# A node loop's edge products two trips behind, with the split in two buffers and the sum in mid-trip

## The chip, the core and the metric

One NeuronCore of a Trainium2 chip runs the whole kernel. The metric is the time of one execution on the device, in microseconds (us). Engines: PE is TensorE (PEld its weight loads), DVE is VectorE, ACT is ScalarE, POOL is GpSimd, SP is SyncE, which here only issues transfers (SPq). L1472 is line 1472 of the kernel's file.

## The reference

Two layers of a graph network on 100,000 nodes of 64 features and 50,000 edges, fp32. Cut to what matters:

```python
h = relu(layernorm(x))
agg = segment_sum(h[src] * edge_weight[:, None], dst)
x = x + agg @ W_neigh + b_neigh + h @ W_self.T
seg_sum, seg_max, cnt = ...        # of edge_attr (32 wide), over src
seg_mean = seg_sum / max(cnt, 1);  seg_max = where(cnt > 0, seg_max, 0)
h = relu(concat([seg_sum, seg_max, seg_mean, u]) @ W1 + b1)   # hidden width 128
out = x + h @ W2 + b2
```

(The layer norm of the second layer enters nothing: that layer's result depends on the edges' attributes alone.)

## The kernel before, in words

The first three fifths of the program rank the edges, sort them by their source into windows of 128 nodes, gather the source nodes and make the messages; the change does not touch them. They leave in DRAM, for each window of 128 nodes, up to 96 slots of edge attributes sorted by source, per-slot flags, the messages sorted by destination (as three bf16 parts of each fp32 number, whose sum is the number), and x plus its own part.

The node loop (L1389 to L1646) then makes the output. It has WG = 98 trips; a trip g handles GT = 8 windows, 1024 nodes. Each engine runs its own program, and semaphores (`w[...]`) order them. Loads go through rings of four buffers (RING = 4), most other buffers exist once or twice. In trip g:

- SP (L1392 to L1403) loads x of the windows (L1399, one transfer) and eight chunks of messages (L1403, eight transfers), as soon as the buffers of trip g-4 are free: for x that is the semaphore "y" (the sum of g-4 made), for the chunks "picked" (their products made).
- POOL (L1408 to L1422) loads attributes, slots and flags.
- DVE: `permute(g+1)` (L1432, a one-hot of the slots), `value_left(g-1)` (L1478), `picks(g)` (L1460, L1462, the one-hot that adds messages into nodes), `value_low(g-1)` (L1484), `select(g)` (L1450, the one-hot that takes each node's last slot), `scans(g+1)` (L1441, L1442, L1444: running sum, running maximum and mean), `finish(g-1)` (L1472: y = x + PSUM).
- PE: `hidden(g)` (L1554, 24 fp32 products with W1), `permute(g+1)` (L1543), `edges(g-1)` (L1589), `outer(g)` (L1565 and L1568, the products with W2, called output or outer products here), `neighbours(g)` (L1579, the messages).
- ACT: `value_mid(g-1)` (L1633), `relu(g)` (L1622), `store(g-2)` (L1616, issues the store of y), `value_high(g)` (L1629).

The outer products leave an fp32 value in PSUM for each slot. It is split in three bf16 parts, high by ACT, what is left by DVE (`v_left`), mid by ACT, low by DVE, into one buffer `v_part`; then `edges` adds the parts, by 24 selecting products with the one-hot `sel`, to the same PSUM bank (two of them, by g % 2) in which `neighbours(g)` has already put the messages. `finish` reads that bank. So one window's value runs L1568, L1629, L1478, L1633, L1484, L1589, L1472 over two trips, and PE's queue has `edges(g-1)` ahead of `outer(g)`.

The order of the work is written out by hand: the order of calls in each engine's loop. The lines that wait, as they stand:

```python
def neighbours(g):                       # PE
    pe.wait_ge(w["pick"], g + 1)
    if g >= 2:
        pe.wait_ge(w["y"], g - 1)        # the bank's last sum
def select(g):                           # DVE
    if g >= 2:
        dve.wait_ge(w["o_ps"], g - 1)    # sel[g % 2] is read by edges(g-2)
```

Of the kernel before, what the change touches and what calls it, by code (L numbers as in the profile page):

```python
# [17 lines left out]
GT = 8  # L18
# [50 lines left out]
def graph_layers(nc, x, src, dst, attr, weight, w_neigh, b_neigh, w_self, u, w1, b1, w2, b2, out):  # L69
    N, D = x.shape  # L70
# [31 lines left out]
    with ctx:  # L102
# [518 lines left out]
        def parts_of(row):  # L621
            return row.bitcast(BF16).rearrange("p k (s c) -> p k s c", s=PARTS)
# [62 lines left out]
        def self_of(g):  # L685
            return s0_d[g * (GT * P):(g + 1) * (GT * P), :].rearrange("(p k) c -> p k c", p=P)
# [671 lines left out]
        sums, tops, means = (part_of(arena, P, 2 * SL) for _ in range(3))  # L1358
        hid = part_of(arena, P, GT * SL)
        v_left = part_of(arena, SL, GT, D)  # L1360
        v_part = parts_of(part_of(arena, SL, GT, KEY))
        one_hot = [part_of(arena, P, GT, P).rearrange("p k c -> p (k c)").bitcast(BF16)
                   .rearrange("p (n k c) -> p n k c", n=2, c=P) for _ in range(2)]
        sel = [one_hot[b][0:SL, 0, :, :] for b in range(2)]
# [24 lines left out]
        with nc.Block() as block:  # L1389
            @block.sync  # L1390
            def _(sp):

                at = [sp.alloc_register(f"at{k}") for k in range(GT)]
                for g in range(WG):
                    b = g % RING
                    sp.reg_load(at, starts[0:1, 0, g * GT:g * GT + GT])
                    if g >= RING:
                        sp.wait_ge(w["y"], g - RING + 1)
                    sp.dma_start(x_in[b][:, :, :], self_of(g)).then_inc(x_loaded[b], 16)  # L1399
                    if g >= RING:  # L1400
                        sp.wait_ge(w["picked"], g - RING + 1)
                    for k in range(GT):
                        sp.dma_start(chunk[b][0:CH, k, :], message[bass.ds(sp.snap(at[k]), CH), :]).then_inc(ch_loaded[b], 16)  # L1403

            @block.gpsimd
            def _(pool):
# [18 lines left out]
            def _(dve):  # L1425
# [49 lines left out]

                def value_left(g):
                    dve.wait_ge(w["high"], g + 1)
                    nc.vector.tensor_tensor(v_left[:, :, :], ps[v_bank][0:SL, :].rearrange("p (k c) -> p k c", c=D),  # L1478
                                            v_part[:, :, 0, :],
                                            ALU.subtract).then_inc(w["left"], 1)  # L1480

                def value_low(g):
                    dve.wait_ge(w["mid"], g + 1)
                    nc.vector.tensor_tensor(v_part[:, :, 2, :], v_left[:, :, :], v_part[:, :, 1, :],  # L1484
                                            ALU.subtract).then_inc(w["v"], 1)

                def c0_rows():
# [27 lines left out]
                for g in range(WG):  # L1515
                    if g + 1 < WG:
                        permute(g + 1)
                    if g >= 1:
                        value_left(g - 1)
                    picks(g)  # L1520
                    if g >= 1:
                        value_low(g - 1)
                    select(g)
                    if g + 1 < WG:
                        scans(g + 1)
                    if g >= 1:
                        finish(g - 1)
                value_left(WG - 1)
                value_low(WG - 1)
                finish(WG - 1)  # L1530

            @block.tensor
            def _(pe):
# [49 lines left out]
                def edges(g):  # L1583
                    c = g % 2
                    pe.wait_ge(w["sel"], g + 1)
                    pe.wait_ge(w["v"], g + 1)
                    for k in range(GT):
                        for n in range(PARTS):
                            last = nc.tensor.matmul(ps[o_bank[c]][:, D * k:D * k + D], sel[c][:, k, :], v_part[:, k, n, :],  # L1589
                                                    start=False, stop=(k == GT - 1 and n == PARTS - 1))  # L1590
                    last.then_inc(w["o_ps"], 1)

# [2 lines left out]
                for g in range(WG):  # L1595
                    hidden(g)
                    if g + 1 < WG:
                        permute(g + 1)
                    if g >= 1:
                        edges(g - 1)  # L1600
                    outer(g)
                    neighbours(g)
                edges(WG - 1)

            @block.scalar
            def _(act):
# [17 lines left out]

                def value_high(g):
                    act.wait_ge(w["v_ps"], g + 1)
                    if g >= 1:
                        act.wait_ge(w["o_ps"], g)
                    nc.scalar.activation(v_part[:, :, 0, :], ps[v_bank][0:SL, :].rearrange("p (k c) -> p k c", c=D), ACT.Copy).then_inc(w["high"], 1)  # L1629

                def value_mid(g):
                    act.wait_ge(w["left"], g + 1)
                    nc.scalar.activation(v_part[:, :, 1, :], v_left[:, :, :], ACT.Copy).then_inc(w["mid"], 1)  # L1633

                for g in range(WG):
                    if g >= 1:
                        value_mid(g - 1)
                    relu(g)
                    if g >= 2:
                        store(g - 2)  # L1640
                    value_high(g)
                value_mid(WG - 1)
                store(WG - 2)
                store(WG - 1)
                for b in range(RING):
# [241 lines left out]
```

## Time and profile before

| | us |
|---|---|
| median of 3 runs | 1773.02 (1772.13 to 1776.54) |
| the profiled execution | 1769.93 |
| its span in the trace | 1768.0 |
| first to last relu of the node loop (L1622, 98 of them) | 1086.9 to 1746.5 |
| PE busy over the whole span | 1081.4 (61%) |
| DVE busy over the whole span | 1390.8 (79%) |

The trace is of one execution; its busy times are of instructions, and an instruction's time on PE and DVE can overlap the start of the next by some hundredths of a microsecond, so that from start to start is shorter than the duration. The granted clock (PEclk) is 1.00 at TensorE's level of 2.4 GHz and 0.50 at 1.2 GHz. The first 1060 us belong to the parts that are not touched.

### The profile page before, as it was taken

The page shows a single profiled execution, that of the slowest core. Times are in us where ns is not written, and L with a number is a line of the kernel's source. Part 1 is how long each engine was busy: PE and PEld are TensorE (multiplying, and loading weights), DVE is VectorE, ACT ScalarE, POOL GpSimd, SP SyncE. Part 2 cuts the span into 40 slices and gives each one's busy share as a digit, 9 for nine tenths or more (in the row PEclk, how much of TensorE's full clock was granted, in tenths as well). Part 3 has the DMA queues.
Part 4 walks back from the last instruction along what each step waited for, and adds up shares of the span by engine and source line. Part 5 has one row for each costly group of instructions (what it writes and reads, how often), then busy time and mean ns, then how long its engine had stood idle before and what let it go on. Part 6 is the DMA issues. An engine that isn't in the chain of part 4 may idle for free. (4 is left out here: it accounts for less than half of the span.)

```text
span 1768.0 us, 39354 instructions
## 1 busy us (share of the span) xinstructions
PE 1081.4 (61%) x13658; PEld 933.2 (53%) x13659; DVE 1390.8 (79%) x3220; ACT 679.9 (38%) x1766; POOL 1104.8 (62%) x1407
## 2 busy tenths in 40 slices
PE   3266666666651023333333344898989998999996
PEld 2155555555551023332233333777877777777775
DVE  6599999999981056766667666888888988888886
ACT  2278888888840012222222221333333333333332
POOL 7777777777777777777777755444444444444440
PEclk9777788888865555555555556888788888878787
DMA  9944545454531053344432226878887878787882
GB/s 289 169 115 116 128 113 128 115 129 114 130 101 42 15 128 96 104 111 106 108 103 71 85 84 166 211 203 206 198 211 194 211 195 206 206 201 201 203 204 61
DMA packets 433690, 255.33 MB, mean 144 GB/s; under 512 B 373693, under 2 KB 381117, under 8 KB 432813
## 3 DMA queue, kind: packets, MB, share of 16 engines
q1 hardware_dynamic: 283198, 144.42, 33.7%
q0 software_dynamic: 46976, 72.79, 15.8%
q10 hardware_dynamic: 103312, 35.54, 8.0%
q8 instruction: 112, 1.84, 0.4%
q14 instruction: 92, 0.75, 0.1%
HBM read 164.15 MB, written 88.42 MB: 143 GB/s over the span
## 5 line engine op out<-in xcount | busy, mean ns | idle before, releaser
L850 POOL DMA_INDIRECT xg_all<-in_x_dram,idx_src x391 | 397.9, 1018 | 120.1 <-issue 118.9
L856 POOL DMA_INDIRECT by_win<-rows,idx_win x391 | 388.1, 993 | 128.1 <-issue 127.2
L1185 PE MATMUL ps<-ident,h 128*128 128x128 f32 x588 | 139.9, 384 | 279.0 <-DVE h L999 204.9
L1413 POOL DMA_DIRECT2D rows<-by_win x98 | 67.7, 691 | 353.9 <-DVE arena L1444 333.2
L1271 ACT ACTIVATE sq<-xc 128x512 f32<-128x512 f32 x147 | 92.6, 630 | 472.5 <-DVE xc L962 472.4
L1185 PEld LDWEIGHTS ps<-ident,h 128*128 128x128 f32 x588 | 94.7, 198 | 298.9 <-DVE h L999 218.2
L951 DVE TENSOR_REDUCE stat<-xg_all 128x8 f32<-128x512 f32 x49 | 33.4, 682 | 230.4 <-DMA xg_all<-in_x_dram,idx_src 230.3
L1418 POOL DMA_DIRECT2D rows<-flag_d x392 | 193.6, 501 | 12.2 <-issue 12.2
L1289 ACT ACTIVATE h<-xc,stat 128x64 f32<-128x64 f32 x784 | 196.3, 332 | 0.0
L1629 ACT ACTIVATE arena<-ps 96x512 bf16<-96x512 f32 x98 | 58.0, 592 | 332.9 <-PE ps L1568 238.1
L1568 PE MATMUL ps<-w_sb,arena 128*96 128x64 f32 x1568 | 184.1, 281 | 0.0
L1568 PEld LDWEIGHTS ps<-w_sb,arena 128*96 128x96 f32 x1568 | 168.9, 192 | 22.5 <-issue 22.5
L1554 PE MATMUL ps<-arena,w1r 32*128 32x192 f32 x2352 | 159.5, 413 | 9.2 <-DVE arena L1444 9.2
L1198 PE MATMUL ps<-wsT,hT 128*128 128x128 f32 x784 | 148.8, 353 | 1.3 <-DVE zeros L1012 0.8
L1198 PEld LDWEIGHTS ps<-wsT,hT 128*128 128x128 f32 x784 | 139.6, 266 | 2.5 <-issue 2.1
L1589 PE MATMUL ps<-arena 96*128 96x64 bf16 x2352 | 94.7, 201 | 66.9 <-DVE arena L1484 66.9
L1554 PEld LDWEIGHTS ps<-arena,w1r 32*128 32x128 f32 x2352 | 123.4, 234 | 16.0 <-issue 9.6
L1589 PEld LDWEIGHTS ps<-arena 96*128 96x128 bf16 x2352 | 84.7, 104 | 88.1 <-issue 87.9
L1478 DVE TENSOR_TENSOR arena<-ps,arena 96x512 f32<-96x512 f32 x98 | 67.3, 687 | 75.6 <-ACT arena L1629 73.0
L445 PE MATMUL ps<-ones_b,same 128*128 128x1 bf16 x392 | 17.0, 164 | 176.9 <-DVE pos_f L350 176.6
L1462 DVE TENSOR_TENSOR arena<-iota_n,arena 96x1024 bf16<-96x1024 f32 x98 | 119.6, 1221 | 3.4
L1622 ACT ACTIVATE arena<-ps,hbias 128x768 f32<-128x768 f32 x98 | 88.2, 900 | 85.0 <-PE ps L1554 85.0
(209 smaller groups left out, 2580.4 us busy)
## 6 DMA issues: line engine op xcount, KB each, us to landing
rows<-message SPq DMA_DIRECT2D x784, 36.4 KB, 3.3
rows<-flag_d POOLq DMA_DIRECT2D x392, 72.0 KB, 3.6
rows<-s_d SPq DMA_DIRECT2D x98, 256.0 KB, 2.9
out_dram<-rows ACTq DMA_DIRECT2D x97, 256.0 KB
message<-m_row SPq DMA_DIRECT2D x48, 388.0 KB, 2.4
arena<-in_x_dram SPq DMA_DIRECT2D x70, 256.0 KB, 3.4
s_d<-arena SPq DMA_DIRECT2D x70, 256.0 KB, 2.2
zeros<-slot_d POOLq DMA_DIRECT2D x98, 144.0 KB, 3.3
```

The lines of the kernel that those rows point to most:

```text
L850: nc.gpsimd.indirect_dma_start(out=xg[g % RX][:, t % GT, :], out_offset=None, in_=x, in_offset=bass.IndirectOffsetOnAxis(ap=idx_src[:, t:t ...
L856: nc.gpsimd.indirect_dma_start(out=by_win, out_offset=bass.IndirectOffsetOnAxis(ap=idx_win[0:parts, t:t + 1], axis=0), in_=rows[0:parts, t ...
L1185: last = nc.tensor.transpose(hT_of[n % 2][:, P * k:P * k + P], h[n % 2][:, 2 * k:2 * k + 2, :].rearrange("p a c -> p (a c)"), ident[:, :])
L1198: last = nc.tensor.matmul(bank[:, P * k:P * k + P], hT[n % 2][:, k, :], weights[:, :], start=True, stop=True)
L1271: nc.scalar.activation(sq[:, :, :], xc[n % 2][:, :, :], ACT.Square).then_inc(ln["squared"], 1)
L1289: last = nc.scalar.activation(h[b][:, k, :], xc[b][:, k, :], ACT.Relu, scale=stat[b][:, 2, k:k + 1])
L1418: pool.dma_start(f_in[b][DE * q:DE * q + DE, :, :].rearrange("p f s -> p (f s)"), two.unsqueeze(0).to_broadcast([DE, 3 * 2 * SL])).then_in ...
L1462: nc.vector.tensor_tensor(pick[c][0:CH, :, :], iota_n[0:CH, :].unsqueeze(1).to_broadcast([CH, GT, P]), near[c][:, :].unsqueeze(2).to_broad ...
L1554: last = nc.tensor.matmul(ps[z_bank[q]][:, 0:2 * SL], w1r[DE * q:DE * q + DE, j, :], part[DE * q:DE * q + DE, :], start=(j == 0), stop=(j ...
L1568: last = nc.tensor.matmul(ps[v_bank][0:SL, D * k:D * k + D], hid[:, SL * k:SL * k + SL], w2_sb[:, :], start=False, stop=(k == GT - 1))
L1589: last = nc.tensor.matmul(ps[o_bank[c]][:, D * k:D * k + D], sel[c][:, k, :], v_part[:, k, n, :], start=False, stop=(k == GT - 1 and n == ...
L1622: nc.scalar.activation(hid[:, :].rearrange("p (q c) -> p q c", q=4), z_ps, ACT.Relu, bias=hbias[:, :]).then_inc(w["hid"], 1)
```

## The change

`edges` runs two trips behind instead of one: in trip g PE makes the selecting products of g-2, at the same place in its order. `v_part` becomes two buffers, by g % 2, so ACT's value_high(g) waits for the products of g-2 rather than g-1, and DVE's value_left(g) also waits for "v" of g-1, since `v_left` is still one buffer. DVE's `finish` runs for g-2, and stands after value_low and before select instead of at the end of the trip. ACT stores g-3 rather than g-2. SP issues the chunks ahead of x. After the loop stand edges(WG-2), finish(WG-2) and store(WG-3) in addition.

```diff
--- before.py
+++ after.py
@@ -1358,7 +1358,7 @@
         sums, tops, means = (part_of(arena, P, 2 * SL) for _ in range(3))
         hid = part_of(arena, P, GT * SL)
         v_left = part_of(arena, SL, GT, D)
-        v_part = parts_of(part_of(arena, SL, GT, KEY))
+        v_part = [parts_of(part_of(arena, SL, GT, KEY)) for _ in range(2)]
         one_hot = [part_of(arena, P, GT, P).rearrange("p k c -> p (k c)").bitcast(BF16)
                    .rearrange("p (n k c) -> p n k c", n=2, c=P) for _ in range(2)]
         sel = [one_hot[b][0:SL, 0, :, :] for b in range(2)]
@@ -1395,12 +1395,12 @@
                     b = g % RING
                     sp.reg_load(at, starts[0:1, 0, g * GT:g * GT + GT])
                     if g >= RING:
-                        sp.wait_ge(w["y"], g - RING + 1)
-                    sp.dma_start(x_in[b][:, :, :], self_of(g)).then_inc(x_loaded[b], 16)
-                    if g >= RING:
                         sp.wait_ge(w["picked"], g - RING + 1)
                     for k in range(GT):
                         sp.dma_start(chunk[b][0:CH, k, :], message[bass.ds(sp.snap(at[k]), CH), :]).then_inc(ch_loaded[b], 16)
+                    if g >= RING:
+                        sp.wait_ge(w["y"], g - RING + 1)
+                    sp.dma_start(x_in[b][:, :, :], self_of(g)).then_inc(x_loaded[b], 16)
 
             @block.gpsimd
             def _(pool):
@@ -1475,13 +1475,15 @@
 
                 def value_left(g):
                     dve.wait_ge(w["high"], g + 1)
+                    if g >= 1:
+                        dve.wait_ge(w["v"], g)
                     nc.vector.tensor_tensor(v_left[:, :, :], ps[v_bank][0:SL, :].rearrange("p (k c) -> p k c", c=D),
-                                            v_part[:, :, 0, :],
+                                            v_part[g % 2][:, :, 0, :],
                                             ALU.subtract).then_inc(w["left"], 1)
 
                 def value_low(g):
                     dve.wait_ge(w["mid"], g + 1)
-                    nc.vector.tensor_tensor(v_part[:, :, 2, :], v_left[:, :, :], v_part[:, :, 1, :],
+                    nc.vector.tensor_tensor(v_part[g % 2][:, :, 2, :], v_left[:, :, :], v_part[g % 2][:, :, 1, :],
                                             ALU.subtract).then_inc(w["v"], 1)
 
                 def c0_rows():
@@ -1520,13 +1522,14 @@
                     picks(g)
                     if g >= 1:
                         value_low(g - 1)
+                    if g >= 2:
+                        finish(g - 2)
                     select(g)
                     if g + 1 < WG:
                         scans(g + 1)
-                    if g >= 1:
-                        finish(g - 1)
                 value_left(WG - 1)
                 value_low(WG - 1)
+                finish(WG - 2)
                 finish(WG - 1)
 
             @block.tensor
@@ -1586,7 +1589,7 @@
                     pe.wait_ge(w["v"], g + 1)
                     for k in range(GT):
                         for n in range(PARTS):
-                            last = nc.tensor.matmul(ps[o_bank[c]][:, D * k:D * k + D], sel[c][:, k, :], v_part[:, k, n, :],
+                            last = nc.tensor.matmul(ps[o_bank[c]][:, D * k:D * k + D], sel[c][:, k, :], v_part[c][:, k, n, :],
                                                     start=False, stop=(k == GT - 1 and n == PARTS - 1))
                     last.then_inc(w["o_ps"], 1)
 
@@ -1596,10 +1599,11 @@
                     hidden(g)
                     if g + 1 < WG:
                         permute(g + 1)
-                    if g >= 1:
-                        edges(g - 1)
+                    if g >= 2:
+                        edges(g - 2)
                     outer(g)
                     neighbours(g)
+                edges(WG - 2)
                 edges(WG - 1)
 
             @block.scalar
@@ -1624,22 +1628,23 @@
 
                 def value_high(g):
                     act.wait_ge(w["v_ps"], g + 1)
-                    if g >= 1:
-                        act.wait_ge(w["o_ps"], g)
-                    nc.scalar.activation(v_part[:, :, 0, :], ps[v_bank][0:SL, :].rearrange("p (k c) -> p k c", c=D), ACT.Copy).then_inc(w["high"], 1)
+                    if g >= 2:
+                        act.wait_ge(w["o_ps"], g - 1)
+                    nc.scalar.activation(v_part[g % 2][:, :, 0, :], ps[v_bank][0:SL, :].rearrange("p (k c) -> p k c", c=D), ACT.Copy).then_inc(w["high"], 1)
 
                 def value_mid(g):
                     act.wait_ge(w["left"], g + 1)
-                    nc.scalar.activation(v_part[:, :, 1, :], v_left[:, :, :], ACT.Copy).then_inc(w["mid"], 1)
+                    nc.scalar.activation(v_part[g % 2][:, :, 1, :], v_left[:, :, :], ACT.Copy).then_inc(w["mid"], 1)
 
                 for g in range(WG):
                     if g >= 1:
                         value_mid(g - 1)
                     relu(g)
-                    if g >= 2:
-                        store(g - 2)
+                    if g >= 3:
+                        store(g - 3)
                     value_high(g)
                 value_mid(WG - 1)
+                store(WG - 3)
                 store(WG - 2)
                 store(WG - 1)
                 for b in range(RING):
```

## Rows read from the trace of the kernel before

**Rows 1.** One stretch of the loop, PE: us, busy (x instructions), PEclk, DMA share, GB/s

```profile
1100.00:1750.00 650.00, 584.83 (x9991) 0.83 0.79 199
```

**Rows 2.** Waits in 1100 to 1750 us: total us, times, longest

```profile
PE ps L1589 <- DVE arena L1484: 65.3, 63, 1.5
```

**Rows 3.** Timeline, DVE, one trip: start us, us, engine, line

```profile
1423.77 0.69 DVE L1478 TENSOR_TENSOR arena<-ps,arena 96x512 f32<-96x512 f32 x1
...
1425.70 0.68 DVE L1484 TENSOR_TENSOR arena<-arena 96x512 bf16<-96x512 f32 x1
1426.31 1.21 DVE L1450 TENSOR_TENSOR arena<-iota_n,end_n 96x1024 bf16<-96x1024 f32 x1
...
1428.60 0.68 DVE L1472 TENSOR_TENSOR rows<-rows,ps 128x512 f32<-128x512 f32 x1
1429.20 0.62 DVE L1432 TENSOR_SCALAR arena<-zeros,row_n 96x768 f32<-96x768 bf16 x1
```

**Rows 4.** Timeline, DVE, before the loop

```profile
1073.74 0.62 DVE L1432 TENSOR_SCALAR arena<-zeros,row_n 96x768 f32<-96x768 bf16 x1 [12.26 <-DMA rows<-flag_d]
1074.28 0.18 DVE L1488 CAST arena<-c0b 128x64 bf16<-128x64 f32 x1
```

**Rows 5.** Timeline, PE, a trip at the full level and the start of the next

```profile
1421.54 1.57 PE L1568 MATMUL ps<-w_sb,arena 128*96 128x64 f32 x16
...
1423.78 1.26 PE L1554 MATMUL ps<-arena,w1r 32*128 32x192 f32 x24
1424.97 0.54 PE L1543 MATMUL ps<-arena,rows 96*32 96x96 f32 x16
1426.53 0.86 PE L1589 MATMUL ps<-arena 96*128 96x64 bf16 x24 [1.03 <-DVE arena L1484]
...
1427.66 2.21 PE L1568 MATMUL ps<-w_sb,arena 128*96 128x64 f32 x16
```

**Rows 6.** Timeline, ACT, the same trip

```profile
1423.14 0.59 ACT L1629 ACTIVATE arena<-ps 96x512 bf16<-96x512 f32 x1 [3.27 <-DVE rows L1472]
...
1425.11 0.90 ACT L1622 ACTIVATE arena<-ps,hbias 128x768 f32<-128x768 f32 x1
```

**Rows 7.** Stretches of one clock level, PE, columns as in rows 1

```profile
1414.74:1421.56 6.82, 5.79 (x119) 1.00 0.76 200
1421.56:1428.39 6.83, 5.80 (x114) 1.00 0.76 185
1428.39:1435.22 6.83, 6.83 (x95) 0.50 0.80 218
```

**Rows 8.** Timeline, PE, at the low level

```profile
1431.08 2.30 PE L1554 MATMUL ps<-arena,w1r 32*128 32x192 f32 x24
1433.32 0.87 PE L1543 MATMUL ps<-arena,rows 96*32 96x96 f32 x16
...
1749.08 2.70 PE L1568 MATMUL ps<-w_sb,arena 128*96 128x64 f32 x16
1751.58 1.49 PE L1579 MATMUL ps<-rows,arena 97*128 97x64 bf16 x24
1754.67 1.44 PE L1589 MATMUL ps<-arena 96*128 96x64 bf16 x24 [1.60 <-DVE arena L1484]
```

**Rows 9.** Timeline, DVE: the sum L1472 of single trips

```profile
1163.17 0.68 DVE L1472 TENSOR_TENSOR rows<-rows,ps 128x512 f32<-128x512 f32 x1
...
1435.57 0.69 DVE L1472 TENSOR_TENSOR rows<-rows,ps 128x512 f32<-128x512 f32 x1
...
1442.81 0.68 DVE L1472 TENSOR_TENSOR rows<-rows,ps 128x512 f32<-128x512 f32 x1
...
1709.33 0.67 DVE L1472 TENSOR_TENSOR rows<-rows,ps 128x512 f32<-128x512 f32 x1
```

**Rows 10.** SP: the chunks of one trip (timeline), and their landing (page)

```profile
1423.72 4.05 SPq L1403 DMA_DIRECT2D rows<-message  x8
...
rows<-message SPq DMA_DIRECT2D x784, 36.4 KB, 3.3
```

## The prediction

> **What bounds the kernel now.** I read the page first, for where the loop stands: it is the last two fifths of its slices, where DVE and PE are both nearly full and the clock's digits swing. Then the busy time over 650 us of the loop: PE works 585 us of them, nine tenths, at a mean granted clock of 0.83 [rows 1]. No engine is full, so I asked who waits for whom: the selecting products (L1589) wait 63 times, about 1.03 us each, for DVE's last part of the split, L1484 [rows 2].
>
> The timeline of one trip at the full level shows both loops that could set 6.13 us (from one DVE sum, L1472, to the next). One is DVE's own work: from L1478 to the next L1432 it is 5.43 us with no gap [rows 3]; L1432 itself, seen where nothing holds its successor, is 0.54 us from start to start [rows 4]. That makes 5.97. The other is the chain of one window's value: L1484 to L1589 0.83 us, L1589 to L1568 1.13, L1568 to ACT's L1629 1.60, on to L1478 0.63, and over the picks to L1484 1.93 [rows 3, 5, 6]. That makes 6.12. So the chain binds, and DVE stands still some 0.16 us in a trip. PE has 5.11 us of work in it (6.13 less the idle 1.02 between L1543's end and L1589).
>
> Then the clock. It moves between its two levels, 1.2 and 2.4 GHz, in stretches; a low one of 6.83 us lies between high ones, mostly of twice that length. In a high stretch PE is busy 5.8 of 6.83 us, in a low one all of it [rows 7]. At the low level hidden (L1554) takes 2.24 us from start to start for 1.19, the outer products 2.70 us in duration for 1.57, and the whole of PE's trip, by the durations of the low rows, 8.9 us (1.49 + 2.24 + 0.87 + 1.44 + 0.35 for L1565 + 2.50 for L1568) [rows 5, 8]. One low stretch costs two trips 14.21 us for 12.26: 1.95 us [rows 9]. A mean clock of 0.83 says that 34% of the loop is low, so 650 us hold 32 such stretches, about 63 us; 6.13 us a trip plus that gives 6.80, and the trips have it. The loop is thus 0.16 us a trip of chain and about 0.67 of clock above DVE's own 5.97.
>
> One number more decides the forecast. Eighty trips from 1163.17 to 1709.33 take 546.16 us [rows 9]: 6.827 each, equal to the length of the clock's shortest stretch to a part in a thousand. A mean over trips of 6.13, 6.97 and 7.24 has no reason to hit that number unless the trips are held in step with the clock's changes: they run ahead at 6.13, come to stand so that the clock falls, lose 2 us and stand right again.
>
> **The change, part by part.** The selecting products of window g-2 in trip g: their split was finished a trip before, so the 1.02 us of waiting goes, and the chain of the value is cut. What is late next at the full level is DVE: 5.97. The gain there is 0.16 x 97 trips = 15.5 us. The bounds: nothing, if the permutation's 0.54 can't be had here; a few us more, if the waits behind finish cost less.
>
> The sum (L1472) moves to mid-trip and now waits for products of the same trip. Count from L1432's start: left at 0.54, low at 2.47, finish at 3.08, select 3.68, end 5.97, the scans' result at 6.05 [rows 3, 4]. PE starts hidden 0.15 later as it does after L1484 now, at 0.23 of the next trip, then permute at 1.42, the selecting products 1.96 to 2.82: the sum finds them 0.2 us early. Queued behind it are select and the scans, and PE's next hidden waits for those. If the low level falls on that piece: 0.23 + 2.24 + 0.80 + 1.44 = 4.71 [rows 5, 8], the sum is 1.68 us late, with all behind it; working through the next trip gives some 0.2 more. So a low stretch costs about 1.9 us in the new order too, against 1.95 now: the cost changes its place (the chain's wait at L1478 before, the sum after), not its size.
>
> The outer products need hidden's relu: hidden ends 1.42, ACT's mid part ends at about 1.9, relu 0.90 [rows 6] to 2.8, where PE is ready at the same time, so 0 to 0.15 us in PE's slack. neighbours(g) now waits for the sum of the same trip, done at 3.76; PE gets there at 4.5. The second buffer of the split: value_high waits for the products of g-2, which stand ahead of its own input; value_left's wait is for DVE's own earlier work: each nothing, at most 0.05 us of issue, 5 us in all if it were exposed. Covers: PE's place in its queue, and DVE's own order.
>
> SP: the eight transfers of the chunks go ahead of the one of x, and the wait for y behind them. SP's chunks need 4.05 us of a 6 us trip [rows 10]. After the change the sum it waits for (g-4) stands in the middle of trip g-2, so the chunks of g+1 go out from 4.3 of trip g-2 to 2.5 of trip g-1, land 3.3 later [rows 10], and are read at 1.15 of g+1: over a trip spare. x is read a trip later than now. The store (g-3 for g-2) finds its sum done; the old image of y is wanted two and a half trips after. Price: nothing, with a trip of cover on each. POOL's loads hang on permute and scans, which keep their places. At the end one more group of products and one more sum stand behind the last trip, in a PE gap of 1.60 us against their 1.44 [rows 8]: 0 to +0.7 us.
>
> **The sum.** By the trips alone: -15.5 (chain) - 1 (low stretches) + 0.5 (end) = -16. By the trips in step with the clock: a fast trip of 5.97 runs ahead sooner, the clock falls sooner, and it pays until the mean is 6.83 again. That takes 97 x (6.80 - 5.97) / 1.9 = 42 low stretches in the place of 33; nothing is left but where the steps begin and end: -1.5, between -7 and +4. I take this one, since [rows 9] show the step held over 80 trips with an accuracy that a cost per trip would not give. The profiled execution was 1769.93 us with a span of 1768.0; the median of the runs is 1773.02, 3.1 above, and I put the difference on that: 1771.5.
>
> On the clock a page has a say. The rows: in high stretches PE is idle for one gap of about 1.02 us a trip, and the clock falls all the same [rows 5, 7]. The Trainium skill, TensorE: Matmul & The Clock Gate, in its section on the HAM oscillation that comes from cycling through PSUM, says that short idles between groups of products are enough to make the clock swing, and that throughput goes in the swings; these rows agree. Taken further, that rule speaks for the change (fewer idles, fewer falls) and gives the last rival below.
>
> **The rivals.**
> In step (0.52): 1771.5. For it: 6.827. Against: a step that held with 6.13 need not hold with 5.97.
> DVE has no 0.16 to give (0.05): L1432 costs 0.70 in every trip, the fast trip stays 6.13: 1773. Against: [rows 4].
> The clock falls as often as now (0.23): about 33 low stretches, each at 1.9, and fast trips of 5.97: 1757, 1753 to 1760. For it: mean busy shares of PE hardly change. Against: [rows 9].
> The clock is low half the time (0.14): as after some high stretches now, every single high stretch of 6.83 us is followed by a low one, and the sum in mid-trip takes the full loss each time. In 13.65 us then stand (13.65 - 1.95) / 5.97 = 1.96 trips, 6.96 us a trip: 0.14 to 0.16 more than now, 97 times, 1787. It decides from two things together: a mean clock of 0.75 and over 1.75 us lost in a low stretch; at 1.7 it is 6.83 and no change. PE's place is L1589, behind hidden and permute at the low level; DVE's is the wait of L1472, with select and scans queued behind it. A half-paid form is 1778.
> The clock falls less (0.06): idle drops from 1.02 to 0.86 us (5.97 - 5.11) in two pieces. With 22 low stretches: -15.5 - 11 x 1.95 = -37: 1736. The section named above would point here; the chance is small since the idle is hardly less.
>
> **How the numbers follow.** About 0.3%, 5.3 us, is what can be told from no change. In step: 0.42 same, 0.08 faster, 0.02 slower; no 0.16: 0.05 same; falls as now and falls less: 0.29 faster; half low: 0.14 slower. Faster 0.37, same 0.47, slower 0.16. The range takes in the in-step case, the case of unchanged falls and the lighter half of the low-half case: 1755 to 1780; in-step alone would be 1766 to 1777.
>
> **What would show it.** Right: fast trips between two L1472 of 5.97 to 6.0; no wait of L1589 for L1484; new waits of L1472 for L1589; a mean trip of 6.83; mean clock in the loop down from 0.83 to about 0.78. Wrong: mean clock 0.83 with 6.65 us a trip (falls as now), fast trips of 6.13, a trip above 6.9 with the clock at 0.75, or SP's chunks on DVE's list of waits.

## The result, and the profile after

The changed kernel takes 1692.29 us (median of 4, 1687.28 to 1702.37), against 1772.58 of the kernel before: a ratio of 0.955, interval 0.950 to 0.960. That is 80 us less, where the forecast was 1771.5 with a range of 1755 to 1780, in which the change would be paid back by TensorE's clock.

The windows view of the loop, PE alone (us, busy with instructions, granted clock, DMA share, GB/s), answers to [rows 1]:

```profile
1100.00:1680.00 580.00, 500.73 (x10080) 0.99 0.89 222
```

The granted clock is 0.99 where it was 0.83. The clock's line of the page shows it over the whole program: the last two fifths are the loop.

```profile
PEclk9678787787777555555555556599999999999998
```

The timeline of PE in one trip answers to [rows 5]:

```profile
1395.04 1.26 PE L1557 MATMUL ps<-arena,w1r 32*128 32x192 f32 x24 [0.72 <-DVE arena L1444]
1396.23 0.54 PE L1546 MATMUL ps<-arena,rows 96*32 96x96 f32 x16
1396.70 0.87 PE L1592 MATMUL ps<-arena 96*128 96x64 bf16 x24
1397.62 0.41 PE L1568 MATMUL ps<-arena 3*96 3x512 bf16 x1
1397.96 1.57 PE L1571 MATMUL ps<-w_sb,arena 128*96 128x64 f32 x16
1399.37 0.90 PE L1582 MATMUL ps<-rows,arena 97*128 97x64 bf16 x24
1400.99 1.26 PE L1557 MATMUL ps<-arena,w1r 32*128 32x192 f32 x24 [0.72 <-DVE arena L1444]
```

(Lines have moved: hidden is L1557, permute L1546, the selecting products L1592, the outer products L1568 and L1571, neighbours L1582.) The wait ahead of the selecting products is gone. PE's idle now stands in front of hidden, 0.72 us, where it waits for DVE's scans; the trip is 5.95 us, as both L1557 rows show. DVE's sum over the whole loop, the lines view of L1472, answers to [rows 9]:

```profile
L1472 DVE TENSOR_TENSOR rows<-rows,ps x98: 674/676/689, 1101.8 to 1681.7; 128x512 f32<-128x512 f32 x98
```

579.9 us for 97 trips, 5.98 each, against 659.4 before (1096.7 to 1756.1). The whole gain is in the loop. POOL's wait in the rows below stood there before. New are PE's wait for the scans and 13 waits of DVE's picks for a load of messages (late loads, from here on); what the forecast had as the likely new wait, the sum for its products, stays small:

```profile
POOL rows L1413 <- DVE arena L1444: 268.3, 88, 4.2
...
PE ps L1557 <- DVE arena L1444: 72.3, 94, 1.3
...
DVE arena L1460 <- DMA rows<-message: 5.8, 13, 1.3
DVE rows L1472 <- PE ps L1592: 1.9, 2, 1.0
```

Some runs below came to chips on which the parts ahead of the loop take 300 us longer, for every kernel; there the ratios are diluted, and the loop alone (first to last sum) is compared.

### The profile page after: what moved, and what is told of

Its sections match the earlier page's. It is cut to its first block and busy times, and to the rows that moved or that the text cites. A ratio compares the mean times of both kernels' runs of the same rounds, so it can differ in the third digit from the quotient of the medians.

```text
span 1693.7 us, 39358 instructions
## 1 busy us (share of the span) xinstructions
PE 988.4 (58%) x13658; PEld 841.2 (50%) x13659; DVE 1381.0 (82%) x3220; ACT 670.9 (40%) x1766; POOL 1090.5 (64%) x1407
## 5 line engine op out<-in xcount | busy, mean ns | idle before, releaser
L1413 POOL DMA_DIRECT2D rows<-by_win x98 | 51.2, 522 | 300.7 <-DVE arena L1444 279.6
L1557 PE MATMUL ps<-arena,w1r 32*128 32x192 f32 x2352 | 127.2, 347 | 82.3 <-DVE arena L1444 82.3
L1571 PE MATMUL ps<-w_sb,arena 128*96 128x64 f32 x1568 | 155.2, 252 | 0.0
L1571 PEld LDWEIGHTS ps<-w_sb,arena 128*96 128x96 f32 x1568 | 141.7, 166 | 22.5 <-issue 22.5
L1557 PEld LDWEIGHTS ps<-arena,w1r 32*128 32x128 f32 x2352 | 97.6, 190 | 94.5 <-DVE arena L1444 84.8
L1637 ACT ACTIVATE arena<-arena 96x512 bf16<-96x512 f32 x98 | 61.8, 631 | 192.2 <-DVE arena L1480 192.2
L1450 DVE TENSOR_TENSOR arena<-iota_n,end_n 96x1024 bf16<-96x1024 f32 x98 | 118.9, 1213 | 0.0
L445 PEld LDWEIGHTS ps<-ones_b,same 128*128 128x128 bf16 x392 | 14.2, 101 | 182.9 <-issue 182.4
L969 DVE TENSOR_REDUCE stat<-sq 128x8 f32<-128x512 f32 x147 | 99.5, 677 | 2.1 <-ACT sq L1271 2.1
```

What stands on the lines that cost most here:

```text
L969: nc.vector.tensor_reduce(stat[n % 2][:, 3, :], sq[:, :, :], AX, ALU.add).then_inc(ln["summed"], 1)
L1450: nc.vector.tensor_tensor(sel[g % 2][:, :, :], iota_n[0:SL, :].unsqueeze(1).to_broadcast([SL, GT, P]), end_n[:, g * GT:g * GT + GT].unsque ...
L1557: last = nc.tensor.matmul(ps[z_bank[q]][:, 0:2 * SL], w1r[DE * q:DE * q + DE, j, :], part[DE * q:DE * q + DE, :], start=(j == 0), stop=(j ...
L1571: last = nc.tensor.matmul(ps[v_bank][0:SL, D * k:D * k + D], hid[:, SL * k:SL * k + SL], w2_sb[:, :], start=False, stop=(k == GT - 1))
```

## Experiments

### Is the clock the gain? Products that do nothing, in the gap of the kernel before

```diff
                 def edges(g):
                     c = g % 2
+                    if g >= 1:
+                        pe.wait_ge(w["y"], g)
+                    for _ in range(24):        # b_fill24; 8 in b_fill8
+                        nc.tensor.matmul(ps[o_bank[1 - c]][:, 0:D], identb[:, :], identb[:, 0:D], start=True, stop=True)
```

> The kernel before with 24 more bf16 products in PE's gap ahead of the selecting products (results thrown away; they fill about 0.8 of the 1.03 us). Theory G (what changed is PE's idle gap, and with it the granted clock): PE's idle per trip falls under that of the changed kernel, the clock stays high, the chain still gives 6.13 us a trip: mean clock in the loop over 0.97, about 1708 us. Rival S (the order of the queues itself brought the gain: DVE no longer waits on the value): more work on PE brings nothing or costs at the low level: 1773 or up to 1800 us, mean clock 0.83 or less.

> The same with 8 products (0.27 us of the gap filled, 0.75 left, about the changed kernel's 0.72 of one gap). Theory G: if it is the length of the gap or the idle share (12% of a trip) that decides, the clock stays high mostly: 1710 to 1730 us. Rival: 1773 and a mean clock of 0.83.

Measured: 1708.59 us (0.965, 0.963 to 0.966) with 24 and 1705.81 (0.962, 0.961 to 0.964) with 8. With more work on PE the kernel before is 63 and 66 us faster. The windows rows of the loop, with 24 and with 8 products:

```profile
1100.00:1680.00 580.00, 558.32 (x12193) 1.00 0.87 222
```

```profile
1100.00:1680.00 580.00, 514.66 (x10697) 1.00 0.88 223
```

The clock is 1.00, and the fast trip stays at the chain's 6.13 us. With 8 products 0.69 us of idle is left in the old place:

```profile
1408.96 0.86 PE L1593 MATMUL ps<-arena 96*128 96x64 bf16 x24 [0.69 <-DVE arena L1484]
```

So of the 80 us, 66 are the clock and the 13.5 that are left between 1705.8 and 1692.3 are the chain.

### Idle given back to the changed kernel

A fill is a write that nobody reads, on DVE.

```diff
                     if g + 1 < WG:
                         scans(g + 1)
+                    nc.vector.memset(prod[:, 0:4, :], 0.0)      # a_hold_s; 0:8 in a_hold_l
```

> The changed kernel with a DVE fill of 128 elements behind the scans in each trip (0.1 to 0.2 us, which lengthens PE's gap by as much: 0.85 to 0.9 us, a trip of about 6.1). By its own time it costs 10 to 18 us: 1702 to 1710. Theory G: near the edge of the kernel before (1.03 us of gap, 6.13 us trip), clock falls may come back: anything up to 1760. Rival S: 1702 to 1710, clock as in the changed kernel.

> The same with 256 elements (0.25 to 0.3 us a trip; PE's gap 1.0 us, trip 6.22). By its own time 1717 to 1722 us. Theory G: the idle per trip is again that of the kernel before, the clock falls as it did there: mean clock 0.8 to 0.85 in the loop and 1765 to 1785 us, ten times the fill's own cost over the shorter fill. Rival S: 1717 to 1722 and a clock that stays high.

Measured: 1698.32 us (0.958, 0.955 to 0.962) and 1699.68 (0.959, 0.957 to 0.960). The fill of 256 elements made a trip of 6.10, with PE idle 0.72 us ahead of hidden and 0.20 ahead of the outer products, near the kernel before in both, and the clock did not fall (windows row of the longer one):

```profile
1100.00:1680.00 580.00, 494.38 (x9968) 1.00 0.86 222
```

At 0.15 us a trip this fill should cost 14 us, and it costs 7: a_hold_l has no late load left. Theory G as it was put, that the amount of idle decides, missed here. So the next kernels changed the place of the idle.

### The gap in other places of the order

Three reorderings. The first is the kernel before, with the outer products first:

```diff
-                    if g >= 1:
-                        edges(g - 1)
                     outer(g)
+                    if g >= 1:
+                        edges(g - 1)
                     neighbours(g)
```

> The kernel before with one edit: PE issues the outer products of g ahead of the selecting products of g-1 (no lag of two trips, one split buffer, the sum at the trip's end). The value's chain no longer runs through the outer products, so PE need not wait in front of L1589. Theory G: any way to take the gap away keeps the clock high: fast trips of 5.95 to 6.0, mean clock over 0.95, 1690 to 1710 us. Rival S (it takes the lag of two trips and the sum in mid-trip): 1760 us or more.

Measured: 1762.44 us (0.995, 0.993 to 0.997). The chain is cut as well as in the changed kernel, and the fast trip is 6.02 us; but the gap now stands in front of the outer products, which wait for relu. The timeline and the windows row:

```profile
1403.16 0.54 PE L1543 MATMUL ps<-arena,rows 96*32 96x96 f32 x16
1404.71 0.41 PE L1565 MATMUL ps<-arena 3*96 3x512 bf16 x1 [1.01 <-ACT arena L1622]
...
1409.18 0.54 PE L1543 MATMUL ps<-arena,rows 96*32 96x96 f32 x16
1410.73 0.41 PE L1565 MATMUL ps<-arena 3*96 3x512 bf16 x1 [1.01 <-ACT arena L1622]
```

```profile
1100.00:1680.00 580.00, 510.41 (x9018) 0.84 0.81 203
```

Removing the wait for the value is not enough. This trace also shows the step that the forecast counted on: from the 11th sum to the 91st, the same eighty trips as in [rows 9], it takes 544.97 us, 6.812 each, with fast trips of 6.02:

```profile
1167.73 0.69 DVE L1472 TENSOR_TENSOR rows<-rows,ps 128x512 f32<-128x512 f32 x1
...
1712.70 0.69 DVE L1472 TENSOR_TENSOR rows<-rows,ps 128x512 f32<-128x512 f32 x1 [0.73 <-issue]
```

(It is the slowest of the five runs, 10 us above their median, so the others may have left the step in part.)

The second is the changed kernel with the sum at the end of DVE's trip again:

```diff
-                    if g >= 2:
-                        finish(g - 2)
                     select(g)
                     if g + 1 < WG:
                         scans(g + 1)
+                    if g >= 2:
+                        finish(g - 2)
```

> The changed kernel with the sum of g-2 back at the end of DVE's trip, behind the scans. neighbours(g) waits for that sum, so PE stands still some 1.5 us behind the outer products. Theory G: a gap longer than that of the kernel before; the clock falls, 1780 to 1830 us. Rival: PE has time for it at the high clock, trip stays 5.95 to 6.1: 1690 to 1705 us.

Measured: 1843.83 us (1.041, 1.040 to 1.043). neighbours(g) waits for the sum of its own trip, 1.32 us in the timeline, and the clock goes to 0.78:

```profile
1400.89 1.57 PE L1571 MATMUL ps<-w_sb,arena 128*96 128x64 f32 x16
1403.78 1.44 PE L1582 MATMUL ps<-rows,arena 97*128 97x64 bf16 x24 [1.32 <-DVE rows L1472]
```

```profile
1100.00:1680.00 580.00, 502.34 (x8020) 0.78 0.71 181
```

This tells what the third part of the change is for: the lag of two trips without the sum in mid-trip is 4% slower than no change.

### One long gap, or the same idle in pieces

The fill of 512 elements, ahead of the scans (`a_front`) or behind them (`a_back`), in the changed kernel; and the kernel before with its gap split by two products that wait for the picks:

```diff
+                    nc.vector.memset(rest[:, :, :], 0.0)        # a_front
                     if g + 1 < WG:
                         scans(g + 1)
+                    nc.vector.memset(rest[:, :, :], 0.0)        # a_back
```

```diff
                 def edges(g):                                   # b_split
                     c = g % 2
+                    if g >= 1:
+                        pe.wait_ge(w["y"], g)
+                    pe.wait_ge(w["pick"], min(g + 2, WG))
+                    for _ in range(2):
+                        nc.tensor.matmul(ps[o_bank[1 - c]][:, 0:D], identb[:, :], identb[:, 0:D], start=True, stop=True)
```

> The changed kernel with a DVE fill of 512 elements ahead of the scans (some 0.4 us a trip), so that PE's one gap in front of hidden grows from 0.72 to about 1.1 us. By its own time the fill costs about 40 us: 1730. Theory L (one long gap in a trip brings the clock down): falls come back, mean clock in the loop 0.75 to 0.88 and 1780 us or more. Theory T (the total idle of a trip decides, wherever it stands): the same as its twin with the fill behind the scans. Rival (the clock hangs on the order of the products alone): 1730 and a high clock.

> The same fill behind the scans: it delays DVE's part left and so ACT's relu, not hidden, so PE's idle is in two pieces, 0.7 ahead of hidden and 0.4 to 0.5 ahead of the outer products; trip time and total idle as in the twin. Theory L: no gap is as long as a microsecond, the clock stays high, about 1730 us. Theory T: as the twin, 1780 or more if the twin falls.

> The kernel before with two throw-away products in the middle of PE's gap (they wait for the picks, which are done some 0.3 us into it): PE's idle stays at about 0.95 of 1.02 us a trip, but in two pieces of about 0.35 and 0.6. Theory L: the clock stays high, 1706 us as with 8 products in the gap. Theory T: idle as before, clock as before, 1760 to 1773 us.

These three, and a_fill8 below, ran where the kernel before takes 2099.02 us. Ratios: a_front 0.988 (0.984 to 0.993), a_back 0.976 (0.970 to 0.983), b_split 0.999 (0.996 to 1.002). The loops: a_front 626.5 us, a_back 610.1, b_split 661.9, where the kernel before has 659.4. The timeline of a_front has its one gap at 1.21 us, longer than that of the kernel before; the windows row shows a clock that fell little:

```profile
1703.51 1.26 PE L1558 MATMUL ps<-arena,w1r 32*128 32x192 f32 x24 [1.21 <-DVE arena L1444]
```

```profile
1440.00:2010.00 570.00, 462.85 (x9151) 0.98 0.84 212
```

It did fall, though: eight of the trips in this trace take 7.63 us for 6.44, with hidden at the low level behind the gap, and no load is late there. One of the eight:

```profile
1598.06 2.22 PE L1558 MATMUL ps<-arena,w1r 32*128 32x192 f32 x24 [1.21 <-DVE arena L1444]
```

In a_back the idle is 0.72 and 0.46 us of a trip of 6.37, more idle than in the kernel before; the clock is 1.00, and none of its trips is long:

```profile
1701.01 1.26 PE L1558 MATMUL ps<-arena,w1r 32*128 32x192 f32 x24 [0.72 <-DVE arena L1444]
...
1704.00 0.41 PE L1569 MATMUL ps<-arena 3*96 3x512 bf16 x1 [0.46 <-ACT arena L1627]
```

```profile
1440.00:2010.00 570.00, 464.15 (x9410) 1.00 0.85 217
```

And b_split, with 0.43 and 0.38 us of idle on either side of its two products, falls as the kernel before does:

```profile
1706.05 0.22 PE L1589 MATMUL ps<-identb 128*128 128x64 bf16 x2 [0.43 <-DVE arena L1462]
1706.65 0.86 PE L1594 MATMUL ps<-arena 96*128 96x64 bf16 x24 [0.38 <-DVE arena L1484]
```

```profile
1440.00:2010.00 570.00, 526.28 (x8932) 0.82 0.81 203
```

Both theories fall. A gap of 1.21 us in one place costs little of the clock; gaps of 0.4 us in another cost the clock as much as one of 1.03. In these runs, every kernel whose clock is under 0.9 has 0.8 us or more of idle in front of the selecting, the outer or the neighbours' products; with 0.69 us there (b_fill8) the clock holds. In front of hidden 0.72 us brings no fall (a_back) and 1.21 us brings eight short ones (a_front).

### The place of the idle, alone

```diff
                 def hidden(g):
                     pe.wait_ge(w["u"], g + 1)
+                    if g >= 1:
+                        pe.wait_ge(w["left"], g)                # b_left
```

> The kernel before with one more wait: PE's hidden(g) also waits for DVE's part left of g-1. Nothing of the work or of the chain changes; of PE's 1.03 us of idle some 0.8 move from in front of the selecting products to in front of hidden, where the changed kernel has them. Theory P (it is the place of PE's idle in the order of its products that decides, next to the selecting and outer products or in front of hidden; the kernels with 1.2 us in front of hidden kept the clock): the falls go, loop 595 us, 0.963 of the kernel before. Rival (PE has to be given more work or less idle, as the split gap of the kernel before suggests): falls as before, ratio 1.00.

Measured: 1706.31 us (0.963, 0.960 to 0.965). One wait more on PE in the kernel before, no other edit, and 65 us are gone. The timeline: the same trip of 6.13 us, 0.71 us of idle ahead of hidden (the profile names no releaser for it; by the edit it is the added wait) and 0.25 ahead of the selecting products in the place of 1.03 there.

```profile
1402.11 1.26 PE L1556 MATMUL ps<-arena,w1r 32*128 32x192 f32 x24 [0.71 <-issue]
1403.30 0.54 PE L1543 MATMUL ps<-arena,rows 96*32 96x96 f32 x16
1404.09 0.86 PE L1591 MATMUL ps<-arena 96*128 96x64 bf16 x24 [0.25 <-DVE arena L1484]
...
1408.24 1.26 PE L1556 MATMUL ps<-arena,w1r 32*128 32x192 f32 x24 [0.71 <-issue]
```

```profile
1100.00:1680.00 580.00, 489.36 (x9911) 1.00 0.89 221
```

The other half of the pair leaves the place and makes the trip longer: the fill of 512 ahead of the scans in the kernel before.

> The kernel before with the DVE fill of 512 elements ahead of the scans: a fast trip of 6.13 to 6.5 us and a gap in front of the selecting products of 1.1 to 1.4 us. Theory P: the clock falls as before or more often; 1.01 to 1.05 of the kernel before. Rival A (the falls come from how a trip of 6.13 us stands to stretches of 6.83, and the changed kernel with the same fill, at 6.43, was merely out of step): the clock stays high at a trip near 6.45, 0.98 or less.

Measured: 1771.69 us (1.000, 0.999 to 1.001). The fast trip is 6.44 us (1434.83 to 1441.27), that of a_front; the gap in front of the selecting products is 1.03 us again; the clock falls. Rival A, the length of the trip, is out. So is the length of the longest gap: at the same fast trip a_front has the longer one, 1.21 us in front of hidden, and a clock of 0.98.

```profile
1411.61 0.86 PE L1590 MATMUL ps<-arena 96*128 96x64 bf16 x24 [1.03 <-DVE arena L1484]
```

```profile
1434.83 0.67 DVE L1472 TENSOR_TENSOR rows<-rows,ps 128x512 f32<-128x512 f32 x1
1441.27 0.67 DVE L1472 TENSOR_TENSOR rows<-rows,ps 128x512 f32<-128x512 f32 x1
...
L1472 DVE TENSOR_TENSOR rows<-rows,ps x98: 624/675/686, 1099.5 to 1760.7; 128x512 f32<-128x512 f32 x98
```

```profile
1100.00:1680.00 580.00, 506.12 (x8930) 0.86 0.79 202
```

The last row of the sums is the instructive one: 661.2 us for 97 trips, 6.816 each. A fast trip 0.3 us longer costs nothing at all; the clock falls less often for it (0.86). b_split stands at 6.824. (The kernel before has 6.827 over the eighty trips of the forecast and 6.798 over all 97.) So the means agree with trips held in step, as the forecast had it, in three kernels with 0.8 us or more of idle at L1589 and a fast trip shorter than 6.82, and in the profiled run of b_outer_first with 1.01 us at L1565. a_sum_last, whose clock falls too, has 7.47 a trip, and the changed kernel, whose clock hardly does, has 5.98. What holds the means there, the runs don't show.

### SP's queue

```diff
                     if g >= RING:
+                        sp.wait_ge(w["y"], g - RING + 1)
+                    sp.dma_start(x_in[b][:, :, :], self_of(g)).then_inc(x_loaded[b], 16)
+                    if g >= RING:
                         sp.wait_ge(w["picked"], g - RING + 1)
                     ...
-                    if g >= RING:
-                        sp.wait_ge(w["y"], g - RING + 1)
-                    sp.dma_start(x_in[b][:, :, :], self_of(g)).then_inc(x_loaded[b], 16)
```

> The changed kernel with SP's old order (wait for the sum, x, then the eight chunks). My account of SP gave a trip of cover, so 1692 us, within 0.5%. Rival: the chunks, sent behind a later wait, land late for picks (the changed kernel already shows 13 such waits, 5.8 us in all), DVE stands, PE's gap grows and the clock falls now and then: 1700 to 1740 us.

Measured: 1728.31 us (0.977, 0.975 to 0.980): the order of SP's queue is worth 36 us of the changed kernel. The waits view:

```profile
DVE arena L1460 <- DMA rows<-message: 23.7, 38, 1.5
```

38 late loads and 23.7 us where the changed kernel has 13 and 5.8; the loop is 609.8 us for 579.9, with a granted clock of 0.97. SP's own timeline in the changed kernel shows why it is tight:

```profile
1400.38 0.42 SPq L1403 DMA_DIRECT2D rows<-s_d  x1
1401.54 5.12 SPq L1400 DMA_DIRECT2D rows<-message  x8
1406.71 0.42 SPq L1403 DMA_DIRECT2D rows<-s_d  x1
1407.87 6.00 SPq L1400 DMA_DIRECT2D rows<-message  x8
1413.92 0.43 SPq L1403 DMA_DIRECT2D rows<-s_d  x1
```

From x to x it is 6.33 and 7.21 us here, more than a trip of 5.95. These are two slow ones; from 1100 to 1680 us the 94 loads of x stand 6.10 us apart in the mean, still more than 5.95, with single distances from 5.1 to 8.0. What the ring has ahead is used up now and then. So I took x off this queue:

```diff
-                    if g >= RING:
-                        sp.wait_ge(w["y"], g - RING + 1)
-                    sp.dma_start(x_in[b][:, :, :], self_of(g)).then_inc(x_loaded[b], 16)
+                    if g < RING:
+                        sp.dma_start(x_in[b][:, :, :], self_of(g)).then_inc(x_loaded[b], 16)
...
                     if g >= 3:
                         store(g - 3)
+                        if g + 1 < WG:
+                            n = (g + 1) % RING
+                            act.dma_start(x_in[n][:, :, :], self_of(g + 1)).then_inc(x_loaded[n], 16)
```

> The changed kernel with the load of x taken from SP's queue to ACT's, behind the store that frees its buffer. SP's trip is 0.42 us of x, a gap of 0.7 and 5.1 to 6.0 of chunks, over DVE's 5.95, so the chunks fall behind and DVE waits for them 13 times (5.8 us), and the two falls of the clock stand there. Theory Q (SP's queue is the next bound): the waits and the falls go, 5.95 us a trip, 0.950 to 0.953 of the kernel before. Rival (the transfers themselves are at their bound, 0.9 of the DMA engines' time): no change from 0.955.

Measured: 1687.32 us (0.952, 0.949 to 0.955). In its trace no engine waits for a load of messages, and the loop takes 570.9 us where the changed kernel has 579.9:

```profile
L1471 DVE TENSOR_TENSOR rows<-rows,ps x98: 674/675/687, 1103.3 to 1674.2; 128x512 f32<-128x512 f32 x98
```

The interval overlaps with that of the changed kernel, so the two ran side by side:

> The changed kernel itself, beside the next kernel on the same chip, to set the two against each other: 0.955 of the kernel before, single times spread over 15 us.

> The changed kernel with the load of x on ACT's queue again. Theory Q (SP's queue makes the chunks late now and then, and the clock falls there): 4 to 8 us less than the changed kernel beside it, and a narrower spread. Rival: the first run's 5 us were the spread of the changed kernel: no difference.

Measured, where the kernel before takes 2062.09 us: 0.964 (0.960 to 0.968) for the changed kernel and 0.962 (0.960 to 0.964) for x on ACT's queue; medians 1984.27 and 1984.03. There the changed kernel had 2 late loads and not 13. Single times spread over 28 us for the one and 7 for the other, in six and five runs. The sums of the two profiled runs:

```profile
L1472 DVE TENSOR_TENSOR rows<-rows,ps x98: 674/676/689, 1388.9 to 1966.0; 128x512 f32<-128x512 f32 x98
L1471 DVE TENSOR_TENSOR rows<-rows,ps x98: 674/676/689, 1399.7 to 1970.6; 128x512 f32<-128x512 f32 x98
```

The loop takes 577.1 us in the first and 570.9 in the second, as on the other chip; but the loop of the second began 10.8 us later, and the parts ahead of the loop, which no edit touches, hide the gain in these two whole times. The loads' waits are shown to go and the loop to be 6 and 9 us shorter, in one trace each; a gain in the median is not shown, and I don't claim that this kernel beats the changed one.

Eight throw-away products in front of hidden in the changed kernel bring no gain either:

```diff
                 def hidden(g):
+                    if g >= 1:
+                        pe.wait_ge(w["hid"], g)
+                        for _ in range(8):
+                            nc.tensor.matmul(ps[z_bank[0]][:, 256:256 + D], identb[:, :], identb[:, 0:D], start=True, stop=True)
                     pe.wait_ge(w["u"], g + 1)
```

> The changed kernel with 8 throw-away products in PE's gap in front of hidden (0.27 us of 0.72). Its time is set by DVE at the high level, so nothing is gained there; what it can take away are the falls after a late load of messages (two stretches of 3.4 us in the profiled run) and part of the spread of its runs, 1687 to 1702. Theory: 1685 to 1692 us, no fall of the clock in the loop. Rival: the spread is of the loads, not of the clock: same as the changed kernel, 1692 with the same spread.

Measured: 0.967 (0.961 to 0.974), a loop of 586.0 us with 14 late loads. The products took idle away from a clock that was high already. The expectation that it would not fall in the loop missed too: it was low once, for some 13 us from 1810 us on (0.99 over the loop). The changed kernel has two short low stretches in its first trace and one of some 13 us in its second. Three of these four falls come just behind a wait of neighbours(g) for the sum, 0.66 to 0.75 us long, that a delayed trip brings, and one behind 1.30 us of idle in front of hidden (at 1528.77 us). The first of them:

```profile
1308.39 0.90 PE L1582 MATMUL ps<-rows,arena 97*128 97x64 bf16 x24 [0.69 <-DVE rows L1472]
1310.60 2.30 PE L1557 MATMUL ps<-arena,w1r 32*128 32x192 f32 x24 [1.30 <-DVE arena L1444]
```

The kernels with 0.72 us in front of hidden and no late load (a_back, and x on ACT's queue) have no low stretch between their first and last sum.

### DVE, which bounds the trip now

```diff
-                    nc.vector.tensor_tensor(sel[g % 2][:, :, :], iota_n[0:SL, :].unsqueeze(1)...,
-                                            end_n[:, g * GT:g * GT + GT].unsqueeze(2)...,
+                    nc.vector.tensor_tensor(sel[g % 2][:, :, :], iota_nb[0:SL, :].unsqueeze(1)...,
+                                            end_nb[0:SL, g * GT:g * GT + GT].unsqueeze(2)...,
```

(and likewise in picks, with `near` in bf16.)

> The changed kernel with both one-hots (L1450 and L1462, 1.14 us each from start to start) made from bf16 numbers in the place of fp32 ones. If DVE goes faster for it, up to 1 us of the 5.95 goes and the transfers (0.9 of the DMA engines' time) or PE (5.1 us) bound the trip: 5.3 to 5.8 us, 0.92 to 0.945 of the kernel before. If it doesn't (one operand of each is repeated along the last axis): no change, 0.955.

Measured: 1698.93 us (0.962, 0.957 to 0.966). The second case: the instruction takes 1.22 us, for 1.21 with fp32 numbers.

```profile
1403.41 1.22 DVE L1452 TENSOR_TENSOR arena<-iota_nb,end_nb 96x1024 bf16<-96x1024 bf16 x1
```

The Trainium skill, VectorE: DVE Perf Modes, under what auto-detection checks, lets an operation of two tensors go at the double rate only if every tensor is 16-bit with a step of one element. Here one operand is repeated along its last axis. The row agrees with that.

## Why the prediction was wrong, point by point

**What bounds the kernel before: right.** The chain binds the fast trip at 6.13 us and the clock adds 0.67. The gap filled with products gives 6.13 us a trip at a clock of 1.00; the chain cut on top of it gives 5.95.

**The chain, -15.5 us: right.** 1705.8 less 1692.3 is 13.5. The fast trip, forecast 5.97, is 5.95. Of the new waits, PE's for the scans is there (72.3 us in all), and the sum finds its products ready but for 2 times.

**The clock: wrong, and it is the miss.** The step that failed is "a fast trip of 5.97 runs ahead sooner, the clock falls sooner, and it pays until the mean is 6.83 again", with its 42 low stretches in the place of 33. It took the falls as a property of how fast trips run against the clock's stretches. In the runs they go with the order of PE's queue: how much of PE's idle stands ahead of which products. The change moved it from in front of the selecting products to in front of hidden, and the profiled run had two low stretches of 3.4 us in the loop (the one profiled again had one of some 13), a mean clock of 0.99 for the 0.78 of the forecast. b_left made the same move alone and has a clock of 1.00. The observation behind the step was sound (6.827 us in 80 trips; 6.816 and 6.824 in two kernels more), and in the profiled run of b_outer_first, with a fast trip of 6.02, the step did what the forecast says (6.812). The inference was not sound, that it would hold wherever PE's idle comes to stand. I wrote down the new place of the idle while counting the trip, and priced only its amount.

**The rival that pointed the right way** was the last one, "the clock falls less", at 0.06 and 1736 us, from a rule of the Trainium skill (TensorE: Matmul & The Clock Gate, on the second kind of HAM oscillation). Its form with hardly a fall, 97 trips of 5.97 or some 80 us less, is what came, and it was not priced. I held it unlikely since idle went only from 1.02 to 0.86 us. By a_back and b_split the amount was no reason either way: 1.18 us of idle, 0.72 in front of hidden and 0.46 of the outer products, keep the clock; 0.81 in front of the selecting products (in two pieces) lose it.

**SP: wrong in its size.** "Price: nothing, with a trip of cover on each" came from one trip of 4.05 us of chunks, and that trip was a quick one. From 1100 to 1680 us the eight chunks take 3.9 to 5.9 us in the kernel before, median 4.6, and 3.9 to 6.0 in the changed one, median 4.65. What changed is the trip to which SP must keep up: its own 6.10 us, x and the gaps included, are over DVE's 5.95. "SP's chunks on DVE's list of waits" stood among the forecast's signs of being wrong, and they came. The old order of SP's queue would have cost 36 us. This part of the change, which I took for bookkeeping, is needed.

**PE's low trip of 8.9 us** has L1565 at 0.35, which is its time at the full level; at the low one it is 0.58 in b_outer_first. The sum is nearer 9.1, and nothing in the forecast rests on it.

**The sum in mid-trip: its need was not seen.** I counted that neighbours(g) finds the sum at 3.76, which holds, but did not say what the sum's old place would give: 1843.8 us.

## What to carry to other kernels

Where TensorE's granted clock swings in a loop that has little idle, look where in its queue the idle stands before pricing anything; moving it cost one wait here (b_left), and a few products that do nothing tell within one run whether the clock is the prize. A mean trip that equals a stretch of the clock can mean that small costs and savings don't show for as long as the falls go on (b_hold), not that they must go on. And a reordering that shortens a trip by a few per cent can make a queue that kept up before (here SP's, 6.1 us against 5.95) the next bound.

## What was not expected of the hardware

One idle piece of 1.21 us in a trip of 6.44 (a_front) left the granted clock at 0.98, while two of about 0.4 us in one of 6.13 (b_split) left it at 0.82, with the same products in both but for two small ones. Why 0.7 us of idle in front of hidden is harmless and 0.8 us beside the selecting and outer products is not, these runs don't tell: the two kinds differ in type (fp32 in four row groups against bf16 and fp32 over the whole array) and in what stands next to them, and I made no kernel that takes these apart. Nor is there a run between 0.72 and 1.21 us in front of hidden. A DVE fill that makes every fast trip 0.3 us longer can be free (b_hold, 1.000, 0.999 to 1.001). Eight transfers on SP's queue took 3.9 to 6.0 us for the same bytes in the changed kernel.
